# Self-attention of a decoder block: query product in three f32r passes, and the projection bias added to the residual rows by GpSimd

## The reference, cut to what matters

```python
q = jnp.einsum('bthc,oc->btho', xh, Wq) * scale
k = jnp.einsum('bthc,oc->btho', xh, Wk) * scale
v = jnp.einsum('bthc,oc->btho', xh, Wv)
scores = jnp.einsum('bihc,bjhc->bhij', q, k)
attn = jax.nn.softmax(jnp.where(j > i, -jnp.inf, scores), axis=-1)
y = jnp.einsum('bhij,bjhc->bihc', attn, v).reshape(b, t, d)
x = _layernorm(x + y @ Wu.T + bu)
```

## Time and profile before

| | us |
|---|---|
| median of 3 runs | 1570.85 (1570.66 to 1572.43) |
| the profiled execution | 1572.29 |
| its span in the trace | 1570.6 |
| PE busy in the span | 1492.5 |
| DVE, ACT, POOL busy | 811.3, 602.6, 539.1 |

### The profile page before, as it was taken

The page is one execution under the profiler, slowest core; times in us unless marked ns, Lnnn a source line. Parts: engine busy times, 40 slices in busy tenths (PEclk is TensorE's granted clock), DMA queues, the critical chain, the costliest instruction groups (busy, mean ns, idle before and its releaser), DMA issues. The chain is left out here.

```text
span 1570.6 us, 32655 instructions
## 1 busy us (share of the span) xinstructions
PE 1492.5 (95%) x12242; PEld 1327.8 (85%) x12242; DVE 811.3 (52%) x1851; ACT 602.6 (38%) x1882; POOL 539.1 (34%) x426
## 2 busy tenths in 40 slices
PE   7999999999699999999999859999999999999897
PEld 3577777766598999999999759999999999999785
DVE  4478888877455656656666453222112222122487
ACT  4477777775234444444444231111111111111232
POOL 2455545544455566566566202000000000000254
PEclk9999999998899999999999979999999999999998
DMA  5122323251227433433433050000000000000453
GB/s 179 37 66 83 94 84 91 86 161 56 75 99 203 152 129 133 155 121 134 158 118 133 24 161 24 21 12 12 12 12 23 12 12 12 12 12 1 147 163 119
DMA packets 71596, 130.90 MB, mean 83 GB/s; under 512 B 7218, under 2 KB 15410, under 8 KB 71540
## 3 DMA queue, kind: packets, MB, share of 16 engines
q1 hardware_dynamic: 71540, 130.17, 26.4%
HBM read 106.30 MB, written 22.02 MB: 82 GB/s over the span
## 5 line engine op out<-in xcount | busy, mean ns | idle before, releaser
L401 ACT ACTIVATE a_p<-a_ps_s,a_nmax 112x224 f32<-112x224 f32 (+1 forms) x512 | 198.3, 416 | 96.6 <-DVE a_nmax L467 96.6
L617 POOL TENSOR_TENSOR a_p<-a_p,a_rinv 112x896 f32<-112x896 f32 (+1 forms) x128 | 164.8, 1308 | 174.9 <-DVE a_rinv L475 169.2
L1555 POOL MEMSET o_mhalf<- 128x1 f32 x1 | 0.1, 98 | 506.7 <-POOLq L1114 506.7
L1271 ACT ACTIVATE f_gate<-f_ps_gate,f_bias 128x224 f32<-128x224 f32 x192 | 75.3, 444 | 194.1 <-PE f_ps_gate L1234 194.1
L1070 POOL TENSOR_TENSOR x_cx_lo<-s_cx_raw,x_cx_hi 125x512 fp32r<-125x512 f32 x96 | 120.6, 1284 | 73.4 <-ACT x_cx_hi L901 73.4
L1064 POOL TENSOR_TENSOR x_ct_lo<-s_ct_raw,x_ct_hi 128x750 fp32r<-128x750 f32 x64 | 118.7, 1883 | 12.4 <-ACT x_ct_hi L875 12.4
L277 PEld LDWEIGHTS a_ps_t<-identity,a_p 112*112 112x112 f32 x768 | 87.2, 135 | 34.5 <-issue 13.5
L482 DVE COPY a_pt<-a_ps_t 112x448 f32<-112x448 f32 x128 | 79.4, 621 | 67.5 <-PE a_ps_t L277 67.4
L401 ACT ACTIVATION_READ_ACCUMULATOR a_p<-a_ps_s,a_nmax 112x1 f32 x512 | 113.8, 222 | 0.0
L1305 DVE TENSOR_TENSOR f_xt_lo<-f_ps_x,f_xt_hi 128x448 fp32r<-128x448 f32 x16 | 10.0, 624 | 194.7 <-ACT f_xt_hi L1262 194.7
L277 PE MATMUL a_ps_t<-identity,a_p 112*112 112x112 f32 x768 | 107.0, 262 | 0.0
(11 more groups left out here) (221 smaller groups left out, 4043.9 us busy)
## 6 DMA issues: line engine op xcount, KB each, us to landing
s_ct_raw<-in_ct SPq DMA_DIRECT2D x16, 1500.0 KB, 7.9
s_cx_raw<-in_cx SPq DMA_DIRECT2D x16, 1500.0 KB
a_xt<-in_xt SPq DMA_DIRECT2D x16, 448.0 KB, 3.9
a_xrow<-in_x SPq DMA_DIRECT2D x16, 448.0 KB, 3.6
a_xres<-in_x SPq DMA_DIRECT2D x16, 448.0 KB, 4.6
x_scratch<-a_xn SPq DMA_DIRECT2D x16, 448.0 KB, 3.1
s_x_raw<-x_scratch SPq DMA_DIRECT2D x16, 448.0 KB, 3.7
x_scratch<-x_xn SPq DMA_DIRECT2D x16, 448.0 KB, 6.2
```

The costliest lines, as they stand in the source:

```text
L401: e = act.activation((p1 if c else p0)[:, g, h, :], src, ACT.Exp, bias=nmax[:, g % 2, c, h:h + 1], accum_out=rsum[:, g % 2, c, h:h + 1])
L617: pool.tensor_tensor(p[:, g, :, :], p[:, g, :, :], inv, ALU.mult).then_inc(norm_done, 1)
L1271: a = act.activation(gate[:, j, m, :], region(3 * half + j, k2), ACT.Tanh, bias=bias[:, j, m:m + 1], scale=0.5 if j < 2 else 1.0)
```

## The change

The query product is made in three f32r passes (`a_hi` by `xs_hi`, `a_lo` by `xs_hi`, `a_hi` by `xs_lo`). `a_hi` and `a_lo` are made once by ACT and DVE. The halves `xs_hi`, `xs_lo` of x are made by POOL for each z, by a copy and a subtraction of 448 columns (`halves`), in g = 1 and g = 3. A wait for the loaded columns, `columns_ready`, stands ahead of `normalise` in odd steps. The bias pass is gone; POOL adds the bias, loaded once to all rows (`bu_all`), in place to the residual rows of batch b - 1 in g = 0 and g = 2 of batch b, right behind `normalise` (`with_bias`). DVE's `residual` now waits for that. POOL's loop takes two batches a turn.

```diff
             def z(m, odd, j, landed):
-                wait(pe, xt_in[odd], 16 * landed)
+                wait(pe, xs_done, m + 1)
                 wait(pe, yl_done, 2 * m - 4)
                 wait(pe, zc_done, m)
-                mm = pe.matmul(ps_z[:, 0:2 * T], a_diag[:], xt[:, odd, 2 * j:2 * j + 2, :], start=True, stop=True)
+                for i, (a, x) in enumerate(((a_hi, xs_hi), (a_lo, xs_hi), (a_hi, xs_lo))):
+                    mm = pe.matmul(ps_z[:, 0:2 * T], a[:], x[:, j, :, :], start=(i == 0), stop=(i == 2))
...
-                products = [(two_rows_r[:], bu_split[:])]
+                products = []
...
-                    base = 7 if g % 2 == 0 else 0
+                    base = 6 if g % 2 == 0 else 0
...
-                    w(5, 7)
+                    w(5, 6)
...
-                wait(dve, xres_in[odd], 16 * landed)
+                wait(dve, xb_done, TC * b + c + 1)
                 dve.tensor_tensor(r[:, c, :], ps_w[0:R, :], xres[:, odd, c, :], ALU.add).then_inc(r_done, 1)
...
+            def columns_ready(m, odd, landed):
+                wait(pool, xt_in[odd], 16 * landed)
+                wait(pool, z_done, m - 1)
+            def halves(m, odd, j):
+                src = xt[:, odd, 2 * j:2 * j + 2, :]
+                pool.tensor_copy(xs_hi[:, j, :, :], src).then_inc(xs_rounded, 1)
+                wait(pool, xs_rounded, m + 1)
+                pool.tensor_tensor(xs_lo[:, j, :, :], src, xs_hi[:, j, :, :], ALU.subtract).then_inc(xs_done, 1)
+            def with_bias(b, odd, c, landed):
+                wait(pool, xres_in[odd], 16 * landed)
+                pool.tensor_tensor(xres[:, odd, c, :], xres[:, odd, c, :], bu_all[:], ALU.add).then_inc(xb_done, 1)
...
-            def steps(b):
+            def steps(i, odd):
+                b = 2 * i + odd
                 for g in range(NG):
                     n = NG * b + g
+                    if g % 2 == 1:
+                        columns_ready(2 * b + 2 + g // 2, 1 - odd, i + odd + 1)
                     normalise(n - 1, (g - 1) % NG)
                     if isinstance(n, int):
                         early(n)
+                    if g % 2 == 0:
+                        with_bias(b - 1, 1 - odd, g // 2, i + odd)
+                    if g == 1:
+                        halves(2 * b + 2, 1 - odd, 0)
                     if g == 3:
+                        halves(2 * b + 3, 1 - odd, 1)
                         power(b - 2)
```

More of the change, by code:

```diff
@@ L67, in self_attention @@
         w_lo = sb("w_lo", [128, KC, D], F32R)
[L68 to L71, removed]
+        a_hi = sb("a_hi", [128, 128], F32R)
+        a_lo = sb("a_lo", [128, 128], F32R)
+        xs_hi = sb("xs_hi", [128, 2, 2, T], F32R)
+        xs_lo = sb("xs_lo", [128, 2, 2, T], F32R)
+        bu_all = sb("bu_all", [R, D])
         xt = sb("xt", [128, 2, NG, T])
@@ L103, in self_attention @@
         const_ready = sem("const_ready")
+        ident_done = sem("ident_done")
         bias_in = sem("bias_in")
@@ L114, in self_attention @@
         bu_in = sem("bu_in")
+        xs_rounded = sem("xs_rounded")
+        xs_done = sem("xs_done")
+        xb_done = sem("xb_done")
         prep_id = sem("prep_id")
@@ L199, in _ @@
                 sp.dma_start(wv_diag[C * g:C * g + C, C * g:C * g + C], io["wv"]).then_inc(diag_in, 16)
-            sp.wait_ge(const_ready, 2)
-            for row in (0, 32):
-                sp.dma_start(bu_raw[row:row + 1, :], io["bu"].rearrange("(a d) -> a d", a=1)).then_inc(bu_in, 16)
+            sp.dma_start(bu_all[:], io["bu"].rearrange("(a d) -> a d", a=1).to_broadcast((R, D))).then_inc(bu_in, 16)
             with nc.allow_non_contiguous_dma(reason="biases by partition"):
@@ L226, in _ @@
         def _(pe):
-            pe.wait_ge(const_ready, 8)
+            pe.wait_ge(const_ready, 5)
             pe.wait_ge(w_in, 2 * G * 16)
@@ L341, in early @@
                     job(KB + n - 2, slot)
-            pe.wait_ge(prep_act, 1)
+            pe.wait_ge(prep_dve, 1)
             z(0, 0, 0, 1)
+            pe.wait_ge(ident_done, 1)
             def steps(i, odd):
@@ L355, in w @@
                             early(n, first)
-                        first, last = (min(base + i, 1 + 3 * KC) for i in (first, last))
+                        first, last = (min(base + i, 3 * KC) for i in (first, last))
                         if first < last:
@@ L386, in _ @@
             act.wait_ge(prep_mm, 1)
-            act.wait_ge(const_ready, 8)
+            act.wait_ge(const_ready, 5)
             for g in range(G):
@@ L391, in _ @@
             a.then_inc(prep_act, 1)
+            act.wait_ge(prep_act, 1)
+            act.activation(a_hi[:], a_diag[:], ACT.Copy).then_inc(prep_act, 1)
             def exp(n, g, heads):
@@ L518, in norm @@
                        .then_inc(xn_done, 1)
-            dve.wait_ge(const_ready, 9)
+            dve.wait_ge(prep_act, 2)
+            dve.tensor_tensor(a_lo[:], a_diag[:], a_hi[:], ALU.subtract).then_inc(prep_dve, 1)
+            dve.wait_ge(const_ready, 6)
             dve.wait_ge(bias_in, 32)
@@ L579, in _ @@
         def _(pool):
+            def columns_ready(m, odd, landed):
+                if not within(m, PAIRS):
+                    return
+                wait(pool, xt_in[odd], 16 * landed)
+                wait(pool, z_done, m - 1)
+            def halves(m, odd, j):
+                if not within(m, PAIRS):
+                    return
+                src = xt[:, odd, 2 * j:2 * j + 2, :]
[3 more added lines that the diff above has]
+            def with_bias(b, odd, c, landed):
+                if not within(b, B):
+                    return
+                wait(pool, xres_in[odd], 16 * landed)
+                pool.tensor_tensor(xres[:, odd, c, :], xres[:, odd, c, :], bu_all[:], ALU.add).then_inc(xb_done, 1)
             pool.memset(wv_diag[:], 0.0).then_inc(const_ready, 1)
-            pool.memset(bu_raw[:], 0.0).then_inc(const_ready, 1)
             pool.memset(a_diag[:], 0.0).then_inc(const_ready, 1)
-            pool.memset(two_rows[:], 0.0).then_inc(const_ready, 1)
             pool.memset(identity[:], 1.0).then_inc(const_ready, 1)
             pool.memset(mask[:], 0.0).then_inc(const_ready, 1)
+            columns_ready(0, 0, 1)
+            halves(0, 0, 0)
             pool.memset(mhalf[:], -0.5).then_inc(const_ready, 1)
-            pool.wait_ge(const_ready, 7)
+            pool.wait_ge(const_ready, 5)
             pool.affine_select(out=identity[:], in_=identity[:], compare_op=ALU.is_equal, fill=0.0, base=0,
@@ L592, in _ @@
             pool.wait_ge(prep_id, 2)
[L593 to L597, removed]
+            pool.tensor_copy(identity_b[:], identity[0:R, 0:R]).then_inc(ident_done, 1)
             pool.memset(ones[:], 1.0).then_inc(const_ready, 1)
-            pool.wait_ge(const_ready, 9)
+            pool.wait_ge(const_ready, 6)
+            halves(1, 0, 1)
+            pool.wait_ge(bu_in, 16)
             def early(n):
@@ L632, in steps @@
                         early(n)
+                    if g % 2 == 0:
+                        with_bias(b - 1, 1 - odd, g // 2, i + odd)
+                    if g == 1:
+                        halves(2 * b + 2, 1 - odd, 0)
                     if g == 3:
+                        halves(2 * b + 3, 1 - odd, 1)
                         power(b - 2)
[L636 to L642, removed]
+            for b in range(4):
+                steps(b // 2, b % 2)
+            with pool.Fori(2, B // 2 - 1) as i:
+                for odd in range(2):
+                    steps(i, odd)
+            for b in range(B - 2, B + 2):
+                steps(b // 2, b % 2)
 def cross_attention(nc, io, x1, x2, raw, raw_in, shared):
```

7 lines of the change are left out of this document (removed).

## The result

| | kernel before | changed kernel |
|---|---|---|
| median of the runs | 1570.76 us (4 runs, 1569.34 to 1572.43) | 1582.57 us (4 runs, 1580.58 to 1585.37) |
| ratio | | 1.0076, 95% interval 1.0058 to 1.0094 |
| profiled execution, its span | 1572.29, 1570.6 us | 1585.37, 1583.7 us |

The change makes the kernel 11.8 us slower; the forecast was 1582.5. The page of the changed kernel answers the earlier trace rows. Its lines give the busy time and share of each engine, and the granted clock of TensorE in 40 slices.

A forecast was written before the change was run, and what follows sets the result against it. It took PE to bound steady self-attention, with DVE nearly full in one half batch. Batches +3.9, start -1.1, stall +9.1, clock +0.7, end -0.95: +11.7 on 1570.85, 1582.5 us; own range 1575 to 1589, with rivals 1567 to 1589.

The forecast's parts named there:

- the two mechanisms in it: DVE and POOL excluding each other in g = 0 of steady batches, and PE stopping in batch 14 for late residual rows.
- The lock (part 3): In g = 0, POOL's addition delays DVE's second a_xn by 1.06 us and PE's first projection pass by 0.74 us.
- its bounds: POOL's start may have less time ahead of it in every other batch: 0.3 to 0.5 us in place of 0.74.
- Its other bound: DVE's veps at 208.06 may wait for POOL's subtraction ending at 208.2, 0.15 us more.
- PE's saving (part 1): Bias pass removed 0.23 us, z in three passes 0.15 us: 0.38 us each half batch, 0.77 a batch.
- Net per batch: Steady self-attention batch: +0.74 us in the half batch with the lock, -0.38 in the other, net +0.36.
- The stall (part 4): Batch 14: POOL waits for batch 13's residual rows, so normalise and PE's transposes wait; z +9.1 us, bounds 6.2 to 12.
- rival B: The lock costs as forecast, but batch 13's rows land sooner, so no longer stall: 1572.7 us; chance 0.09.
- The clock: PE's half-clock stretch after the stall lasts as long or somewhat longer: +0.7 us, between -1 and +3.
- Start and end (part 5): Batches 0 to 2, without norm, save 1.1 us; the end behind the stall saves 0.95 us.
- A (no lock): The stall comes, but the lock between DVE and POOL costs PE nothing: 1569.3 us; chance 0.16.
- C (PE the bound everywhere): PE bounds everywhere except its present stall, so every pass removed shows: -11.3 us, 1559.5 us; chance 0.10.

The follow-up runs named there:

- experiments 1 to 3: Changed kernel with: 1, both bias additions in g = 2, 1573.47 us; 2, late rows issued before the cross-attention's loads, 1570.86 us; 3, both of these, 1561.73 us.
- experiments 9, 10: Changed kernel with both edits, plus: 9, first projection pass issued twice, 1570.61 us, or fourth twice, 1564.77 us; 10, z as one float32 product, no halves, 1566.32 us.
- experiment 6: Changed kernel with z as one float32 product again, without halves and columns_ready, so only the bias part: 1584.93 us, ratio 1.0086.
- second pair: Changed kernel and kernel before, both unaltered, run and profiled again: spans 1581.7 and 1566.1 us; changed kernel measured 1582.86 us, ratio 1.0081.
- experiment 7: Changed kernel with POOL's bias additions left out, so only the part with z: 1572.13 us, ratio 1.0025.
- both edits: Changed kernel with both additions in g = 2 and batch 15's columns and batch 13's rows issued before the cross-attention's loads: 1561.73 us, ratio 0.994.
- experiment 8: Changed kernel with both edits, and seven projection passes in the odd step, five in the even one, instead of six and six: 1562.43 us, ratio 0.9947.

## Why the prediction was right, and where only by its sum

The number came out (1582.5 forecast, 1582.57 measured), and the two mechanisms in it are shown by experiments 1 to 3. That it came within 0.1 us is luck: terms that were too large and too small cancel, and the two pairs of profiles alone differ by 2.5 us (13.1 and 15.6). Point by point:

**The lock (part 3)** is as it was put: the second `a_xn` at 1.51 us (212.40 to 213.92, 1.52, in the forecast's order of turns), the copy after it without idle time, PE's first pass later. From the scores of the odd step to PE's first pass it was 1.16 us before (213.30 to 214.46), it is 1.78 now (213.34 to 215.12): +0.62 where 0.74 was forecast. In every other batch it is +0.51 (1.66 now), for POOL's pair has 0.17 us of idle time ahead of it there and not 0.40; the forecast had this among its bounds. Its other bound, that `veps` may wait for the subtraction, is right in kind (last section), but costs `veps` nothing in the steady batches. The Trainium skill ("SBUF — State Buffer", section on who interferes with whom) has it that whoever comes first holds the shared pair for the whole instruction; by that rule the trace agrees, with 0.28 us between the ends. The rows add who is first after a release: the waiting DVE instruction, each time.

**PE's saving (part 1)** failed in size. The price of z was right (0.62 us start to start, 0.60 forecast). But 0.38 us in each undisturbed half batch was forecast, and 0.11 came in the batch shown: 10.59 us against 10.70. On average it is 0.14 (10.55 against 10.69), which is what z saves; of the bias pass nothing came. The step that failed is "PE fills all of 50 us, so self-attention is bound by PE": a PE that is 100% busy can stand in a balance with another engine's chain, and the bias pass stood in the part of the half batch where the chain through ACT's exponentials is as long (experiments 9, 10). No number in the forecast gave that chain.

**Net per batch** +0.25 was measured, +0.36 forecast. The forecast has +0.74 in the half batch with the lock and -0.38 in the other; measured, on average, are +0.39 and -0.14. Both terms were too large, and against each other. That z's saving buys nothing in the half batch with the lock is as forecast: it takes 11.05 us without the three passes (experiment 6) and 11.06 with them. The bias pass (0.23) lies behind the wait for `residual`, where it would have counted, but the wait for the exponential took it back, which the forecast did not know.

**The stall (part 4)** has the right place, order and releaser. Its size was 9.1 us forecast. z came 9.8 us later, but batch 14 began 1.8 later already, and of the 8.0 left, 1.2 are half clock (5.0 us forecast from the transposes to z, 6.16 measured). So the term is 6.8. In the second pair z came 14.3 us later (366.47 against 352.20), 3.9 of them before batch 14 and 1.6 by the clock, so there it is 8.8. What was off is the landing: the rows took 13.5 us from their issue (341.57 to 355.09; 13.5 in the second profile too), not 15.2, for the same transfers as in the earlier trace rows. Counted from the issue of the first of the large loads it is 25.2 us (329.92 to 355.09) where the forecast has 27.4 (328.06 to 355.46). What was missed is that POOL has a second wait of this kind, `columns_ready`. Had the rows of batch 13 come in time, as in rival B, PE would still have lost 9.0 us, as in experiment 7: rival B's price of 1572.7 has no such wait in it.

**The clock** was booked at +0.7. In the first pair it was -1.8: before, the clock was at half for 6.0 us of work and cost 3.0; after, most of the half clock fell into the idle time and cost 1.2. In the second pair the kernel before lost nothing, and the changed one 1.6 (from the transposes at 359.88 to z at 366.47 6.59 us, for the same 5.0). So this term alone lies between -1.8 and +1.6.

**Start and end (part 5).** The start lies within what the pairs scatter, -1.0 and +1.1 up to batch 3. The end behind the stall was not measured by itself.

So self-attention gave +6.9 us in the first pair and +15.6 in the second, where +11.7 was forecast, and the forecast hits the median. In the first pair 6.2 us came from the stages behind, where the clock is granted lower for a longer time (0.78 from 930 to 960 us against 0.99, 0.94 from 960 to 980 against 1.00). I have no experiment on that and leave it open; the distance from the last `a_xn` to the end was 1160.7 to 1166.9 us over all profiles of these kernels, and 1160.7 was the kernel before's.

**The other rivals.** A (no lock) is refuted by the 1509 ns. C (PE the bound everywhere) is refuted even where its conditions hold: with both edits the lock and the stall are gone, and a batch takes 21.10 us where C has 20.6.

## What to carry to other kernels

Before work is taken off a full engine, measure the chain of the others over the same stretch: a pass removed is worth the smaller of its length and the room up to that chain, and doubling a pass at two places shows which chain holds. When a step gets a new wait for a transfer, look through the engine's whole queue for what stands behind it, for every batch in which the transfer is late and for every new wait, not only the first one found. Work that is moved to an idle engine belongs where no instruction of another engine has to wait for it; here the same two additions cost 0.52 us a batch beside DVE's `norm` and nothing in the third step.

## What the runs showed of the hardware

A `tensor_scalar` of 112x512 that met an addition on POOL took 1.51 us in place of 0.54, and the addition 1.47 in place of 1.28: between two instructions of POOL the waiting DVE instruction gets its turn, and POOL's next one pays for it.

A `tensor_scalar` of 112x2 (`veps`, 168 ns alone) waits too, if the subtraction on POOL lasts long enough beside it. Timelines of DVE and POOL in the changed kernel, in an early batch and in a steady one:

```profile
100.14 0.24 DVE L512 TENSOR_SCALAR a_veps<-a_mv 112x2 f32<-112x2 f32 x1
...
208.22 0.17 DVE L512 TENSOR_SCALAR a_veps<-a_mv 112x2 f32<-112x2 f32 x1
```

```profile
99.22 1.14 POOL L596 TENSOR_TENSOR a_xs_lo<-a_xt,a_xs_hi 128x448 fp32r<-128x448 f32 x1
...
207.19 1.14 POOL L596 TENSOR_TENSOR a_xs_lo<-a_xt,a_xs_hi 128x448 fp32r<-128x448 f32 x1
```

At 208.22 they overlap for 0.11 us, and `veps` takes its usual time. At 100.14 they overlap for 0.22, and it takes 243 ns and ends 25 ns behind the subtraction, as in two more batches. In the kernel of experiment 8 this happened in all 13 batches with an overlap: 187 to 244 ns, each ending 22 to 26 ns behind POOL.

The same 448 KB behind the same 3 MB took 13.5 to 15.4 us to land; in the kernel before, PE's wait of 3.81 us was followed by half the clock and that of 2.51 us was not. The spans of these two executions differ by 4.5 us; that the rest of the spread of its runs comes from there was not tried. Three passes of 448 columns in halves take 0.20 us each, 0.62 to the next other pass; with them PE's part of the half batch is 0.14 us shorter than with the one float32 product (4.22 against 4.36).
